# First layer of a two-layer kernel: the attention mask as a spare row of keys and queries, the first norm's rows on ScalarE, another cyclic order

## The reference

```
x = x + L0_xattn(layernorm(x), ctx, mask)   # 16 heads of 16, keys and values from ctx (64 x 128 x 192)
x = x + L0_ffn(layernorm(x))                # switch layer: 8 experts, capacity 512 tokens
x = x + L1_xattn(layernorm(x), ctx)         # 16 heads, no mask
x = x + L1_ffn(layernorm(x))                # six attention nodes of 8 heads

# in L0_xattn
scores = einsum(q, k) * 0.25
scores = where(context_mask[:, None, None, :], scores, -max)
attn = softmax(scores); out = einsum(attn, v) @ Wo
```

## Time and profile before

| | |
|---|---|
| median of 3 runs | 4091.06 us (4090.85 to 4096.52) |
| the profiled execution | 4089.82 us, of it span of the trace 4088.0 us |
| TensorE busy | 4001.1 us, 98% |
| VectorE, ScalarE, GpSimd busy | 2392.3, 2622.6, 1930.2 us |
| mean granted TensorE clock | 0.992 of full speed |
| first layer | first scores at 21.86 us, last round of scores at 605 us, experts from about 650 us |

### The profile page before, as it was taken

The page is one execution under the profiler, slowest core; times in us unless marked ns, Lnnn a source line. Parts: engine busy times, 40 slices in busy tenths (PEclk is TensorE's granted clock), DMA queues, the critical chain, the costliest instruction groups (busy, mean ns, idle before and its releaser), DMA issues.

```text
span 4088.0 us, 100757 instructions
## 1 busy us (share of the span) xinstructions
PE 4001.1 (98%) x38276; PEld 3410.6 (83%) x38276; DVE 2392.3 (59%) x6184; ACT 2622.6 (64%) x11786; POOL 1930.2 (47%) x2011
## 2 busy tenths in 40 slices
PE   8999999999999999999999999999999999999997
PEld 6888886668888888888888888888888888888886
DVE  5777772025566656666666666666665666666553
ACT  6888881215666666666666666666666666666664
POOL 5888883113444444444444444444444444444443
PEclk9999999999999999999999999999999999999999
DMA  3232214521000000000000000000000000000000
GB/s 104 70 97 70 67 53 138 181 73 35 14 13 16 15 14 14 13 14 17 14 13 13 14 13 13 20 12 12 12 12 12 12 12 12 12 12 12 7 4 9
DMA packets 117866, 129.73 MB, mean 32 GB/s; under 512 B 12006, under 2 KB 110676, under 8 KB 117264
## 3 DMA queue, kind: packets, MB, share of 16 engines
q1 hardware_dynamic: 105648, 109.80, 8.4%
q0 software_dynamic: 6144, 8.43, 0.7%
q10 hardware_dynamic: 5600, 5.07, 0.4%
HBM read 89.68 MB, written 41.94 MB: 32 GB/s over the span
## 4 chain that ended last, share of the span: by engine, by line
PE 76%; DVE 1%; ACT 0%; issue 0%; POOL 0%; POOLq 0%; ACTq 0%
PE c_product L1411 37%; PE c_product L1422 15%; PE c_product L1470 11%; PE c_scores L1460 7%; PE c_product L1493 5%; PE c_product L1481 2%; DVE c_qT L1266 1%; PE c_product L1399 1%; ACT c_probs L1223 0%; PE c_product L1530 0%; ACT c_front_probs L1223 0%; DVE c_nodes L1266 0%; DVE c_neg_max L1275 0%; POOL c_probs L1177 0%; DVE c_nodes L1337 0%
## 5 line engine op out<-in xcount | busy, mean ns | idle before, releaser
L1177 POOL TENSOR_TENSOR c_probs<-c_probs,c_row_inv 128x512 f32<-128x512 f32 x768 | 794.9, 1043 | 1390.4 <-DVE c_row_inv L1278 1384.4
L1223 ACT ACTIVATE c_probs<-c_scores,c_neg_max 128x128 f32<-128x128 f32 x3072 | 1084.3, 407 | 354.0 <-DVE c_neg_max L1275 353.9
L1411 PE MATMUL c_product<-c_nodes,cell_w 128*128 128x256 f32 x4352 | 1067.4, 384 | 4.8 <-DVE c_nodes L1266 3.1
L1411 PEld LDWEIGHTS c_product<-c_nodes,cell_w 128*128 128x128 f32 x4352 | 797.4, 190 | 123.7 <-DVE c_nodes L1266 11.8
L1223 ACT ACTIVATION_READ_ACCUMULATOR c_probs<-c_scores,c_neg_max 128x1 f32 x3072 | 759.3, 247 | 0.0
L1275 DVE TENSOR_REDUCE c_neg_max<-c_scores 128x4 f32<-128x512 f32 x1024 | 658.3, 679 | 169.5 <-PE c_scores L1460 161.7
L1229 ACT COPY c_probsT<-c_product 128x512 f32<-128x512 f32 x768 | 419.8, 600 | 462.2 <-PE c_product L1470 458.2
L1223 ACT ACTIVATE c_front_probs<-c_scores,c_neg_max 128x128 f32<-128x128 f32 x1024 | 364.7, 394 | 170.2 <-DVE c_neg_max L1275 170.2
L1422 PE MATMUL c_product<-cell_w,c_nodes 128*128 128x256 f32 x1792 | 430.3, 381 | 0.0
L432 ACT ACTIVATE a_probs<-a_scores,a_neg_max 128x128 f32<-128x128 f32 x1024 | 361.2, 399 | 83.9 <-DVE a_neg_max L488 83.2
L1470 PE MATMUL c_product<-consts_sb,c_probs 128*128 128x128 f32 x3072 | 404.1, 275 | 5.4 <-POOL c_probs L1177 5.4
(11 more groups left out here) (167 smaller groups left out, 6450.2 us busy)
## 6 DMA issues: line engine op xcount, KB each, us to landing
e_w<-in_L_ffn_w SPq DMA_DIRECT2D x12, 1024.0 KB, 6.2
a_x<-in_x SPq DMA_DIRECT2D x32, 256.0 KB, 2.9
a_ctxT<-in_ctx_pairsT SPq DMA_DIRECT2D x32, 256.0 KB, 3.1
x<-a_x SPq DMA_DIRECT2D x32, 256.0 KB, 2.1
xn<-a_xn SPq DMA_DIRECT2D x32, 256.0 KB, 2.2
c_routed<-xn SPq DMA_DIRECT2D x32, 256.0 KB, 2.7
c_x<-x SPq DMA_DIRECT2D x32, 256.0 KB, 3.1
c_ctxT<-in_ctx_pairsT SPq DMA_DIRECT2D x32, 256.0 KB, 2.8
```

The costliest lines, as they stand in the source:

```text
L1177: nc.gpsimd.tensor_tensor(e, e, rinv[:, i, r].unsqueeze(2).broadcast_to([P, 4, T]), ALU.mult).then_inc(norm_made, 1)
L1223: a = nc.scalar.activation(probs(n)[:, r, k], S[r][:, k], ACT.Exp, bias=nmax[:, i, r, k:k + 1], accum_out=rsum[:, i, r, k:k + 1])
L1411: i = T_.matmul(m[:, u], w[:, k, u * P:(u + 1) * P], src[:, k], start=n == 0, stop=n == last)
```

## The change

Three edits in `phase_first_layer`. The mask: `mk` now makes two bf16 tiles `mask_rows` of zeros, with 0 or -2^127 in one spare row of each strip, row 16 for the even head and row 0 for the odd; K's copies add these rows to the keys, Q's copy is done twice (`qT_even`, `qT_odd`), each with a one in the spare row, and the score products, now closed one by one, carry the mask. The four mask products of each round are gone. MASK_JOBS goes from 4 to 2, so masks are loaded and made twice as often, half as large. The first norm's rows: VectorE negates the mean, GpSimd multiplies it by the reciprocal root (`shift`), and ScalarE computes x * rstd + shift with two Identity activations per job. The four tables are new; ROW_RING goes from 6 to 7.

```
              np.full((P, 2), 1e-5), np.full((P, 2), 1e-6)]
+    for row in (16, 0):
+        spare = (i % 32 == row)[:, None]
+        parts += [spare * NEG, ~spare * 0.25, spare]
     return np.concatenate([np.asarray(a, np.float32) for a in parts], 1)
...
 FIRST_PE_ORDER = """
-K:1 T0.1:3 S1:2 Tx:1 A:3 r.n:6 Q:1 O:3 T1.0:2 T0.0:2 S0:1 V:1 L:5 Tn:4 T1.1:2
+Q:1 A:3 T0.0:2 T0.1:2 S0:1 Tn:5 K:0 r.n:6 O:3 V:1 T1.0:2 S1:1 Tx:0 L:5 T1.1:2
 """
 
 FIRST_DVE_ORDER = """
-r.oh:5 S0.i0:1 K^:0 S0.i1:1 S1.x0:1 Tx^:0 S1.x1:1 S1.x3:1 S1.i0:1 A^:2 r.n^:5 S1.x2:1 S1.i1:1 Q^:0 S1.i3:1
-O^:2 S0.i3:1 S1.i2:1 st1:2 S0.i2:1 S0.x0:0 S0.x1:0 S0.x3:0 V^:0 L^:4 r.sh:4 mk:-1 st:-1 S0.x2:0 Tn^:3
+S1.i3:2 st:0 S0.x2:1 S0.x3:1 S0.x0:1 Tn^:5 r.n^:6 S1.i1:2 mk:0 K^:0 S0.x1:1 O^:3 S0.i0:1 V^:1 st1:3 S1.x0:1
+S0.i3:1 S1.x2:1 Tx^:0 S1.i0:1 L^:5 S1.x3:1 r.sh:5 S0.i1:1 S0.i2:1 S1.x1:1 S1.i2:1 Q^:0 r.oh:5 A^:2
 """
 
 FIRST_ACT_ORDER = """
-S1.e1:1 S1.e3:1 S1.e2:1 T1^0:1 T1^1:1 T0^0:1 T0^1:1 S0.e0:0 S0.e1:0 S0.e3:0 r.ex:4 T1^2:1 S0.e2:0 T1^3:1
-T0^3:1 T0^2:1 S1.e0:0
+nm:3 T1^0:5 T1^1:5 S1.e0:4 T1^2:5 S1.e2:4 r.ex:8 T1^3:5 S1.e1:4 S1.e3:4 T0^0:4 T0^1:4 T0^3:4 T0^2:4 S0.e2:3
+S0.e0:3 S0.e3:3 S0.e1:3
 """
 
 FIRST_POOL_ORDER = """
-rs:1 nm:1 rs1:4 S0.n0:2 nm1:4 S0.n1:2 S1.n0:2 S1.n1:2 S1.n3:2 S1.n2:2 S0.n3:2 S0.n2:2 put:9
+S1.n3:1 S1.n1:1 rs:-1 S0.n0:0 S1.n2:1 rs1:2 nm1:2 S0.n3:0 S0.n1:0 S0.n2:0 S1.n0:0 put:8
 """
...
-    X_RING, ROW_RING, GROUP = 4, 6, 4
-    MASK_JOBS, SENDS, RING = 4, 3, 3
+    X_RING, ROW_RING, GROUP = 4, 7, 4
+    MASK_JOBS, SENDS, RING = 2, 3, 3
     plan = cell_plan()
...
-        one_row = sb("one_row", [P], BF16)
+        mku, mkr = sb("mask_u8", [2, MASK_JOBS * W2], U8), sb("mask_rows", [2, MASK_JOBS * W2], BF16)
...
                 elif n == "rs":
                     rsqrt(0, j)
+                    pool.wait_ge(rstd_made[0], j + 1)
+                    nc.gpsimd.tensor_tensor(shift[:, j % 2], neg_mean[:, j % 2], rstd[:, 0, j % 2], ALU.mult).then_inc(shift_made, 1)
-                elif n == "nm":
-                    if j >= 1:
-                        pool.wait_ge(prod, n_prod["Tx", j - 1])
-                    normal(xt[:, j % X_RING], xn, 0, j, xn_made)
...
+                elif n == "nm":
+
+                    act.wait_ge(shift_made, j + 1)
+                    if j >= 1:
+                        act.wait_ge(prod, n_prod["Tx", j - 1])
+                    for b in range(PAIR):
+                        k = nc.scalar.activation(xn[:, b], xt[:, j % X_RING, b], ACT.Identity, bias=shift[:, j % 2, b:b + 1],
+                                                 scale=rstd[:, 0, j % 2, b:b + 1])
+                    k.then_inc(xn_made, 1)
...
+                if i == 0:
+                    k.then_inc(mean_made, 1)
+                    dve.wait_ge(mean_made, j + 1)
+                    k = V.tensor_scalar(neg_mean[:, j % 2], mv[:, 0, j % 2, :, 0], -1.0, None, ALU.mult)
...
                 elif n == "mk":
                     g = j // MASK_JOBS
                     dve.wait_ge(m_in[g % 2], 16 * (g // 2 + 1))
-                    V.tensor_scalar(mkb[:, g % 2], mku[:, g % 2], 1.0, NEG, ALU.subtract, ALU.mult).then_inc(mask_made, 1)
+                    for h in range(2):
+                        spare = cst[:, C_SPARE + 3 * h:C_SPARE + 3 * h + 1]
+                        k = V.tensor_scalar(mkr[:, h], mku[:, g % 2], spare, spare, ALU.mult, ALU.subtract)
+                    k.then_inc(mask_made, 1)
                 elif n == "st":
                     dve.wait_ge(x_in[s], 16 * (j // X_RING + 1))
                     statistics(xt[:, s], 0, j)
                 elif n == "Tx^":
                     V.tensor_copy(xT[:], product(n, j)).then_inc(prod_used, 1)
                 elif n == "Q^":
-                    V.tensor_scalar(qT[:, o], product(n, j), 0.25, None, ALU.mult).then_inc(prod_used, 1)
+                    m = product(n, j)
+                    for h, q in enumerate((qE, qO)):
+                        c = C_SPARE + 3 * h + 1
+                        k = V.tensor_scalar(q[:, o], m, cst[:, c:c + 1], cst[:, c + 1:c + 2], ALU.mult, ALU.add)
+                    k.then_inc(prod_used, 1)
                 elif n == "K^":
                     m = product(n, j)
-                    V.tensor_scalar(kE[:, o], m, cst[:, C_EVEN:C_EVEN + 1], None, ALU.mult)
-                    V.tensor_scalar(kO[:, o], m, cst[:, C_ODD:C_ODD + 1], None, ALU.mult).then_inc(prod_used, 1)
+                    dve.wait_ge(mask_made, j // MASK_JOBS + 1)
+                    t0 = j % MASK_JOBS * W2
+                    for h, (a, c) in enumerate(((kE, C_EVEN), (kO, C_ODD))):
+                        k = V.scalar_tensor_tensor(out=a[:, o], in0=m, scalar=cst[:, c:c + 1], op0=ALU.mult, op1=ALU.add,
+                                                   in1=mkr[:, h, t0:t0 + W2].unsqueeze(1).broadcast_to([P, 2, W2]))
+                    k.then_inc(prod_used, 1)
...
                     b = int(n[1])
-                    pe.wait_ge(mask_made, j // MASK_JOBS + 1)
-                    for r in range(ROWS):
-                        if (n, j) in round_before:
-                            n0, j0 = round_before[n, j]
-                            pe.wait_ge(exp_made, n_exp[f"{n0}.e{r}", j0])
-                        g = slice(32 * r, 32 * r + 32)
-                        off = (PAIR * (j % MASK_JOBS) + b) * T
-                        T_.matmul(S[r][:], one_row[g],
-                                  mkb[g, j // MASK_JOBS % 2, off:off + T].unsqueeze(1).broadcast_to([32, 4, T]),
-                                  start=True, stop=False)
                     landed("Q", j)
                     landed("K", j)
                     for k in range(4):
-                        u, w = k // 2, (kE, kO)[k % 2]
+                        u, q, w = k // 2, (qE, qO)[k % 2], (kE, kO)[k % 2]
                         for r in range(ROWS):
+                            if k == 0 and (n, j) in round_before:
+                                n0, j0 = round_before[n, j]
+                                pe.wait_ge(exp_made, n_exp[f"{n0}.e{r}", j0])
                             g = slice(32 * r, 32 * r + 32)
-                            i = T_.matmul(S[r][:, k], qT[g, o, u, b * T:(b + 1) * T], w[g, o, u, b * T:(b + 1) * T],
-                                          start=False, stop=k == 3)
+                            i = T_.matmul(S[r][:, k], q[g, o, u, b * T:(b + 1) * T], w[g, o, u, b * T:(b + 1) * T],
+                                          start=True, stop=True)
```

17 lines of the change are left out of this document (6 added, 11 removed).

## The result

The changed kernel took 4142.57 us (median of 4 runs, 4138.71 to 4147.59) against 4090.95 us before (4 runs, 4089.68 to 4096.52): ratio 1.0127, 95% interval 1.0115 to 1.0139. The forecast was 4075, its range 4058 to 4094. On a later chip the same program took 4109.38 us (ratio 1.0046, 1.0029 to 1.0063), on another 4146.80 (1.0137, 1.0118 to 1.0156), while the kernel before stayed at 4090 to 4093 on every chip. Two things need a cause: 33 to 37 us that come on some chips only, and 18 us that come on all.

The account below looks back on a forecast made before the run. The prediction took TensorE, busy 98% of the span, as the bound. It summed 31 jobs x -0.4 = -12, start-up -4 and tail 0 to -16, so 4091 - 16 = 4075 us, range 4058 to 4094.

Parts of the forecast that it names:

- The new order, step by step: First layer's S0-to-S1 chain: 7.4 us beside TensorE's 7.6 to 8.0, 0.3 to spare; mk adds a 1.1 us wait.
- Queues: SP's load of x waits for GpSimd's second norm four jobs earlier; x lands at 4.5, needed at 5.2, slack 0.7 us.
- D: Rival, slower: x lands 1.5 us later than 2.7 throughout, +0.4 us a job, 4099 us; chance 0.15.
- Ordinary iterations: First layer without routing: 16.9 us, and 18.0 with mk, so 17.4 a job, 0.4 less than 17.8.
- Routing and the clock behind it: Every fourth job: 4.0 us extra per four jobs, lower clock included, with a 2.5 us TensorE wait in T0.
- The norm on ScalarE: Two Identity activations of 256 columns a job: 0.43 us each, 0.85 a job, hidden behind O, V and T1.0.
- Mask rows: VectorE's two mask rows of 512 columns per two jobs: 0.67 us each, both in 1.3; bounds 0.41 and 0.83.
- Q and K copies: VectorE: two Q copies with pointer scalars at 0.80 us; K copies with the mask row at 0.77, bounds 0.74 and 1.26.
- Start: Start-up: statistics no longer behind the mask, first scores at 18.7 us, exponentials at 20.9 instead of 25.2, 4.3 earlier.
- Forecast A: The main forecast for the whole kernel: 4075 us, counted as met from 4066 to 4084; chance 0.50.
- Rival B: More gained: mask rows 0.41 us each, wait before S1 0.5, clock 2.4 GHz through the routing gap; 4060 us, chance 0.18.
- C: Rival: VectorE's K copies above 0.82 and mask rows at 0.83 give the gain back, only start-up left; 4086 us, chance 0.17.

Follow-up runs that it names:

- e10: The changed kernel once more, without any edit, on a chip without late updates: 4109.38 us, ratio 1.0046 to the kernel before.
- e11: The changed kernel with the mean negated by a one-element reduction instead of tensor_scalar, on a chip without late updates: 4100.60 us, 1.0027.
- e14: The kernel before with only GpSimd's put moved two row scalings earlier, ahead of S0.n3 and S0.n2: 4120.46 us, ratio 1.0066.
- e18: The changed kernel with GpSimd's put behind S1.n3, waiting for the last completion of the running S0 round: 4117.35 us, ratio 1.0060.
- e1: The changed kernel with the mean negated by a one-element reduction instead of tensor_scalar, first run: 4104.77 us, ratio 1.0029.

## Why the prediction was wrong

Cut into stretches, in us, with the forecast by its own terms (-4.3 at the start, then -0.4 a job, which the prediction rounds to -16). A group is four jobs, from the S0 of job 8 (167.87 before) to that of job 28 (543.79):

```
                          start to job 8   five groups, each   rest     sum
forecast against before        -7.5            -1.6            -1.2     -16.7
e10, updates on time           -6.7            +3.5            +7.3     +18.3
e11, the same, reduction       -4.7            +2.2            +4.7     +10.9
changed kernel, first trace    -6.1            +7.8           +15.9     +48.9
```

**The failed step** is in "The new order, step by step": "the first maximum starts 1.08 us after the scores". It was read from a row in which no put ran, and carried to an order in which the put begins with the scores. The "Queues" part asks what SP's loads wait for and does not name the put. Where updates are held the maximum starts at 2.93, 1.65 later than where they are not (1.28), and the chain from S0 to S1 had 0.3 to spare: 18.3 us instead of 16.7, and 19.9 instead of 18.2. That is shown by the same program on chips with and without late updates, by e14 and by e18. (Even on time it is 1.28 and not 1.08.) Fifteen rounds 1.4 to 1.65 us late give at most some 24 of the 33 us; the granted clock is lower too, 0.984 against 0.987 in e10, and the rest was not separated. It is no rival of the four; D, the only slower one, has x late, and the statistics wait for x only 4.0 us in all from 100 to 560 us, 5 times, at most 1.1.

**Ordinary iterations, right where updates are on time**: 16.7 and 18.2 us in turn in e10 and e11, forecast 16.9 and 18.0, with TensorE's wait before S1 of 1.0 (forecast 1.1).

**Routing and the clock behind it, mis-sized: 4.0 us per four jobs forecast, 6.1 to 9.1 measured** in the five groups of e11 (76.0 to 79.0 us, less 70.0 for two ordinary pairs). This is the second step that failed, and the main one where updates are on time: "I leave routing at 4.0 us per four jobs, its lower clock included". The routing iteration itself is 3.7 to 4.1 us above one with mk (once 6.9), much as forecast; but the iteration behind it takes 18.7 to 19.9 us instead of 16.7, where before it took 17.80 like any other (243.14 to 260.94). The stall in T0 is there, 3.5 us five times of six and 2.5 once, forecast 2.5. Of one routing iteration in e11, VectorE and the end of the stall on TensorE:

```profile
389.02 0.88 DVE L583 TENSOR_TENSOR a_gate_probs<-a_exp,a_mx 128x64 f32<-128x64 f32 x1
...
390.19 0.71 DVE L585 TENSOR_TENSOR a_one_hot<-a_gate_probs,a_pm 128x64 f32<-128x64 f32 x1
...
391.71 1.57 DVE L590 TENSOR_TENSOR a_tokens_before<-a_tokens_before,a_one_hot 128x8 f32<-128x8 f32 x8
393.20 0.68 DVE L534 COPY a_oT<-a_product 128x512 f32<-128x512 f32 x1
```

```profile
394.03 0.98 PE L677 MATMUL a_product<-consts_sb,a_probs 128*128 128x128 f32 x4 [3.50 <-DVE a_oT L534]
```

The chain r.oh takes 4.7 us here (to 393.20) where the earlier trace rows had 3.6: two of its operations take 0.88 and 0.71 beside GpSimd's row scalings, and 0.23 and 0.22 in a routing iteration where they don't (469.07 and 469.59). What is left goes with the clock. Two stretches of e11, a routing iteration with a stall of 2.49 and the one behind it (behind the five engines stands the granted clock), then the two parts of them at the lower clock, and TensorE's first product behind each of the two waits:

```profile
448.82:473.96 25.14, 21.34 (x210) 18.28 (x209) 20.54 (x61) 17.32 (x77) 17.91 (x20) 0.84 0.17 54
473.96:492.64 18.68, 18.68 (x214) 16.30 (x213) 14.20 (x40) 16.02 (x74) 11.46 (x15) 0.94 0.20 62
...
459.00:465.80 6.80, 6.80 (x53) 6.38 (x46) 5.09 (x15) 4.86 (x21) 6.26 (x8) 0.50 0.23 67
472.80:476.00 3.20, 3.06 (x37) 2.54 (x37) 1.12 (x6) 1.07 (x2) 1.03 (x1) 0.50 0.02 5
...
458.66 0.39 PE L667 MATMUL a_scores<-front_keys,a_qT_even 32*128 32x128 f32 x3 [1.00 <-ACT a_probs L434]
472.94 1.09 PE L677 MATMUL a_product<-consts_sb,a_probs 128*128 128x128 f32 x4 [2.49 <-DVE a_oT L534]
```

A mean of 0.84 is 32% of the stretch, 8.0 us, at 1.2 instead of 2.4 GHz. Only 1.3 of them lie at the end of the routing stall; 6.8 begin at 459.0, behind mk's wait of 1.00 us before S1 and one of 0.31 (to 456.61), while TensorE works without a pause. So the lower clock came behind short waits too, here and at 271.3 (0.50 from 271.4 to 274.6), though not behind each of them. TensorE is busy 21.34 us there, and 17.86 in a routing iteration of 22.29 us at 0.98 (372.66 to 394.95). The forecast had no row for how long the lower clock lasts.

**How much the clock is worth**, an estimate: the mean granted clock of the profiled executions is 0.992 before, 0.989 in e11, 0.987 in e10 and 0.984 in the first trace after. One less this clock, times the span, is what TensorE's work at the lower level takes longer if it works all that time: 33, 45, 53 and 66 us. So against before e11 loses up to 12 us, e10 up to 21 and the changed kernel up to 33 to the clock, of 10.9, 18.3 and 48.9 in all. Where updates are on time, then, the clock alone is about as large as the whole loss, and takes back what the change gives elsewhere. Which waits bring it down was read from the traces and not tested by a run.

**The norm on ScalarE, mis-sized and harmless**: Identity 0.61 for 0.43. **Mask rows**, mis-sized: 0.52 for the first of a pair and 1.26 for the second, in all pairs but the first (0.55 and 0.54), in e11; 1.78 a pair for 1.3. The prediction read the 0.407 us for 256 columns as nearly one column a cycle; but 512 columns take 0.52, so 256 more cost 0.11 and some 0.3 is fixed (an estimate from these two rows, which are of different types). The 0.3 each that the prediction worked out from the Trainium skill, page "VectorE: DVE Perf Modes", section "The perf-mode tier table", appears in no row: it leaves that fixed part out, while the section's two elements a cycle fit these two rows. **Q and K copies** 0.78 to 0.80 and 0.75: right. **Start**: first scores at 16.9 to 18.4 us (forecast 18.7, before 21.86), and -4.7 to -6.7 at job 8 for -7.5: right in the main.

**The rest**, +4.7 to +7.3, of it 2.0 to 2.3 in the last three jobs and +2.7 to +5.0 behind the last S0, mostly where nothing changed in the code: e11 has a granted clock of 0.86 from 640 to 700 us, before has 0.94. How the first layer's end brings this about was not tested.

Forecast A's figure of 17.4 us a job was reached, then, in ordinary iterations only, and on some chips only. Rival B falls with the mask rows and the clock. C's bound on VectorE did not come either: in e10 it waits 21 times for scores and 55 times for exponentials between 160 and 600 us.

## What to carry to other kernels

A row's delay from one engine to the next belongs to what the other engines do at that moment: when an order is changed, list what will run beside each link of the chain, DMA issues of GpSimd above all, and price the chain with that. Place a GpSimd put where no burst of completions of TensorE ends, by a wait if need be. When a new order adds even short waits of TensorE, look at the granted clock behind them and not only at their length. And compare variants only on one chip, run together: e1 on one chip against the changed kernel on another made a wrong theory look proven, by 38 us.
